# Three PSUM banks for the unit sums of a graph layer, and twelve selection matrices

## The reference

```python
xn = layernorm(x)
gathered = edge_weight[:, None] * xn[dst]                  # graph branch
support = segment_sum(gathered, src, 3125)
graph = relu(concat([xn, support], 1) @ W + b)
mix = mixing(xn)          # logmap, 256 -> 768 projection, batch norm, relu, 32-channel groups,
                          # a linear attention in each node, 512 -> 256 projection, expmap
x = x + graph + mix
x = x + experts(layernorm(x))      # 8 experts, the best two of each node, 256 -> 1024 -> 256
```

## Time and profile before

| | |
|---|---|
| median of 3 runs | 1258.03 us (1256.99 to 1260.42) |
| the profiled execution | 1260.42 us, of which 1260.4 us lie between its first and its last instruction |
| busy | PE 1002.4 us (80%), PEld 810.6, DVE 680.7, POOL 630.3, ACT 598.6 |
| POOL, the 397 gathers (L560) | 394.4 us busy, 994 ns each; idle before them 221.9 us, of it 113.3 for SP's line 455 |
| PE, the unit sums (L705) | 282.1 us busy, 453 ns per instruction; idle before them 164.5 us |

### The profile page before, as it was taken

One profiled execution on the slowest core, in us unless ns is written; L12 is line 12 of the kernel. 1 busy time (PEld: TensorE's weight loads), 2 busy tenths in 40 slices (PEclk: granted clock), 3 DMA queues, 4 the chain that ended last, 5 costly groups with the idle time before them and its releaser, 6 DMA issues.

```text
span 1260.4 us, 21882 instructions
## 1 busy us (share of the span) xinstructions
PE 1002.4 (80%) x5493; PEld 810.6 (64%) x5494; DVE 680.7 (54%) x1493; ACT 598.6 (47%) x1559; POOL 630.3 (50%) x601
## 2 busy tenths in 40 slices
PE   3889579975676777776767557469999999999995
PEld 1456345554555566565655435368999999999995
DVE  8999834432555555555555357943444444444441
ACT  0535234459656676676666445323333343333331
POOL 2473376665666666566666662213433433433431
PEclk8889789996787888789788867778999999999998
DMA  7112222322222222223222343972222222222221
GB/s 157 36 30 84 59 88 88 91 90 80 88 80 87 85 85 88 80 89 90 83 87 85 92 155 122 368 228 48 35 41 35 34 42 34 34 42 34 36 41 18
DMA packets 53869, 103.07 MB, mean 82 GB/s; under 512 B 14923, under 2 KB 36240, under 8 KB 51612
## 3 DMA queue, kind: packets, MB, share of 16 engines
q0 software_dynamic: 30448, 67.69, 21.4%
q1 hardware_dynamic: 22408, 30.48, 7.8%
q10 hardware_dynamic: 932, 3.95, 0.9%
HBM read 83.96 MB, written 18.13 MB: 81 GB/s over the span
## 4 chain that ended last, share of the span: by engine, by line
PE 50%; DVE 14%; another core or an unknown queue 11%; issue 9%; ACT 7%; SPq 3%; DMA 2%; POOL 2%; DVEq 1%; ACTq 0%; POOLq 0%
PE ps L848 15%; PE ps L838 15%; PE ps L705 10%; ACT arena_e L939 3%; PE ps L753 3%; PE ps L716 2%; DVE arena_a L1262 2%; DVE arena_a L1256 2%; DVE arena_c L1343 1%; SPq L454 1%; PE ps L828 1%; POOL arena_c L560 1%; PE ps L648 1%; PE ps L625 1%
## 5 line engine op out<-in xcount | busy, mean ns | idle before, releaser
L560 POOL DMA_INDIRECT arena_c<-y_d,arena_e x397 | 394.4, 994 | 221.9 <-SPq L455 113.3
L705 PE MATMUL ps<-arena_c,arena_e 128*125 x892 | 282.1, 453 | 164.5 <-SPq L458 56.4
L705 PEld LDWEIGHTS ps<-arena_c,arena_e 128*125 128x125 f32 x892 | 184.4, 222 | 243.6 <-issue 218.9
L939 ACT ACTIVATE arena_e<-arena_e 128x125 f32<-128x125 bf16 x446 | 202.3, 509 | 119.2 <-remote 64.6
L1343 DVE TENSOR_TENSOR arena_c<-arena_c,ps 125x256 f32 x223 | 92.6, 415 | 269.2 <-remote 150.3
L592 POOL DMA_INDIRECT out<-node,bn x56 | 100.9, 1802 | 250.8 <-DVE node L1626 225.5
L1065 ACT ACTIVATE arena_d<-ps,small 128x128 f32<-128x128 f32 x448 | 121.5, 382 | 181.8 <-PE ps L838 140.6
L848 PE MATMUL ps<-arena_c,arena_d 128*128 x896 | 205.5, 383 | 0.2 <-issue 0.2
L848 PEld LDWEIGHTS ps<-arena_c,arena_d 128*128 128x128 f32 x896 | 167.9, 192 | 21.7 <-issue 0.6
L838 PEld LDWEIGHTS ps<-node,arena_d 128*128 128x128 f32 x896 | 105.8, 194 | 2.6 <-DVE node L1618 1.2
L838 PE MATMUL ps<-node,arena_d 128*128 128x128 f32 x896 | 106.1, 277 | 0.8 <-DVE node L1618 0.8
(11 more groups left out here) (344 smaller groups left out, 1319.8 us busy)
## 6 DMA issues: line engine op xcount, KB each, us to landing
arena_a<-in_W SPq DMA_DIRECT2D x8, 1024.0 KB, 12.2
arena_c<-y_d,arena_e POOLq DMA_INDIRECT x397
arena_c<-in_W SPq DMA_DIRECT2D x5, 1024.0 KB
arena_c<-in_W ACTq DMA_DIRECT2D x3, 1024.0 KB
x<-in_x SPq DMA_DIRECT2D x5, 560.0 KB
z_d<-x SPq DMA_DIRECT2D x5, 560.0 KB
out<-x SPq DMA_DIRECT2D x5, 560.0 KB
y_d<-arena_c SPq DMA_DIRECT2D x15, 125.0 KB
```

What stands on the lines that cost most here:

```text
L560: pool.indirect_dma_start(ring[:, b % GR, :], None, io["y_d"], bass.IndirectOffsetOnAxis(gix[:, at:at + 1], 0)).then_inc(gth[b % GR], 16)
L705: mm = nc.tensor.matmul(unit_sums(u), sel[(2 * u + j) % SR], ring[:, ds(at + j, 1), :].rearrange("p a c -> p (a c)"), start=(j == 0), stop ...
L939: nc.scalar.activation(sel[b % SR], hot[b // 8 % 2][:, :, b % 8], ACT.Copy, scale=wcols[:, b:b + 1]).then_inc(selm, 1)
```

## The change

From unit 42 on, when the projection no longer needs bank 5, the unit sums rotate through banks 5, 6 and 7, and a unit waits for the add of the unit three before it. `mix_out` gives up bank 5 and writes the columns 256 to 511 of bank 3, whose other half `channel_sums` writes. Two waits go with that: `channel_sums(t)` waits for the store of `mix_out(t-4)`, and `mix_out(t)` waits for the squares of `channel_sums(t+3)`, the one issued last. There are twelve selection matrices in place of eight, and `select` runs eight matrices ahead in place of six. Before unit 42, PE waits until ACT has read the last projection out.

```diff
-SR = 8
+SR = 12
...
-        sel = [cut(T) for _ in range(SR)]
+        sel = [cut(T) for _ in range(8)]
+        cut = cutter(ED[:, 2108:2656])
+        sel += [cut(T) for _ in range(4)]
+        assert len(sel) == SR
...
+        mix_sum = ps[0:T, 3, C:2 * C]
+
         def unit_sums(u):
-            return ps[0:T, 6 + u % 2, 0:C]
+            return ps[0:T, 6 + u % 2 if u < G0 else 5 + (u - G0) % 3, 0:C]
...
-                need(pe, g_acc, u - 1)
+                need(pe, g_acc, u - 1 if u < G0 else u - 2)
...
+            pe.wait_ge(qk_act, OC * 7)
             for u in range(G0, G1):
                 sum_edges(u)
...
             def channel_sums(t):
                 pe.wait_ge(bd_ready, 1)
                 need(pe, a_s, t)
+                need(pe, a_out, t - 3)
...
             def mix_out(t):
                 pe.wait_ge(a_oT, t + 1)
+                need(pe, a_s, min(t + 4, NT))
                 need(pe, a_out, t)
                 for k in range(4):
-                    mm = nc.tensor.matmul(ps[0:T, 5, 0:C], oT[t % 2][:, k, :], wres[:, k, :],
+                    mm = nc.tensor.matmul(mix_sum, oT[t % 2][:, k, :], wres[:, k, :],
...
-            AH = 6
+            AH = 8
...
-                                     ps[0:T, 5, 0:C].rearrange("p (q c) -> p q c", q=4), ACT.Copy).then_inc(a_out, 1)
+                                     mix_sum.rearrange("p (q c) -> p q c", q=4), ACT.Copy).then_inc(a_out, 1)
```

## The result

The changed kernel takes 1267.8 us (median of 4 runs, 1265.68 to 1270.5) against 1257.76 us of the kernel before beside it (1256.99 to 1260.42): ratio 1.0083, 95% interval [1.0058, 1.0108]; a ratio is estimated from the runs and need not be the quotient of the medians. It is 10 us slower, where I forecast 11 us faster. The profiled executions span 1267.5 and 1260.4 us.

What follows compares the result with a forecast made beforehand. The mixing stretch was taken as bound by a circle of waits: POOL, PE, SP and POOL again. 24 - 6 (capped) - 7 = 11 us gained, from 1258.03 to 1247 us; range of 8 in 10: 1224 to 1268.

Steps and rivals of the forecast that it cites:

- The step that failed first: After the last unit: nothing is touched, so gain or loss in the mixing stretch only shifts the experts as a whole.
- rival C: Slower: completions held before both `mix_out` and `channel_sums`, two POOL waits a segment, 50 in all; 1277 us, chance 0.22.
- dry spells: Mixing stretch: POOL's waits for freed slots, 57 of 1.54 us each, 87.9 us, one for 2.7 units.
- The first term, 24 us: Third bank in the mixing stretch: 3.7 units per POOL wait instead of 2.7, 42 waits instead of 57, 24 us less.
- The cap: At `mix_out`: savings between `channel_sums` and `mix_out` can't pass the squares; half of that half kept, so 24 becomes 18 us.
- the wait: `mix_out` waiting for the squares: five tiles lose 2.8 us each, 14 us on PE; bounds 0 and 14, taken as 7.
- rival B: No change: in the mixing segments waiting moves from adds to squares, POOL runs dry 57 times as before; 1258 us, chance 0.16.
- twelve matrices: ACT's selects: more matrices made ahead may let ACT reach its copies sooner; gain taken as 0.
- `channel_sums` waits 1.4 us for the store: `channel_sums` waiting for the store: covered by 0.9 us, taken as 0; at most 39 us if the cover is gone.
- the signs that I named for "right": Mixing stretch: POOL's waits some 45, unit-sum idling well below 117.7 us, `mix_out` idling 1 to 3 us a tile, three units held.
- held completion: Mixing stretch: PE's completions reach nobody for about five microseconds while gathers follow each other, arriving after POOL runs dry.

Runs made afterwards that it cites:

- e8: Changed kernel plus three throwaway matmuls behind each of its last six units and one in each of the first eight logits tiles: 1249.41 us, 0.9977 of the kernel before.
- e5: Changed kernel as it is, run again beside a fresh set of the kernel before: 1259.94 us, ratio 1.0061.
- e14: Changed kernel with mixing sums in bank 4, `mix_out` moved behind the row transposes, and two banks throughout: 1253.72 us, 0.9942 of the kernel before.
- e13: Changed kernel with mixing sums in bank 4, `mix_out` moved, three banks in the mixing segments, two in the tail: 1249.63 us, 0.9900 of the kernel before.
- e7: Kernel before, two banks and eight matrices, with the mixing sums in bank 3 and all the new waits: 1258.76 us, ratio 1.0047.
- e1: Changed kernel plus three throwaway matmuls behind each of its last five units: 1249.42 us, 0.9949 of the kernel before.
- e4: Changed kernel with eight matrices, six ahead, so the third bank and its waits alone: 1261.97 us, 1.0056 of the kernel before.
- e9: Changed kernel with its last 16 units back on two banks, three banks and all waits kept in the mixing segments: 1251.2 us, 0.9977 of the kernel before.
- e11: Kernel before, two banks and eight matrices, with mixing sums in bank 4 and `mix_out` moved behind the row transposes: 1243.63 us, ratio 0.9907.
- e2: Kernel before plus three throwaway matmuls behind each of its last five units: 1251.64 us, ratio 0.9974.
- e3: Kernel before with twelve selection matrices, eight made ahead, and its two banks: 1253.67 us, ratio 1.0003.
- e12: Changed kernel, mixing sums in bank 4, `mix_out` moved, throwaway matmuls behind the last units, in the logits loop and before the experts: 1238.48 us, 0.9869 of the kernel before.

## Why the prediction was wrong

**The step that failed first** is the sentence "The change touches nothing after the last unit; what it gains or loses here shifts the experts as a whole." No instruction after the last unit is changed, but the clock at which they run is: the way from the last add to the first expert takes 10.1 us more, of which the experts give 2.1 back, and the two profiled spans are 7.1 us apart. e8 against e5 shows it by holding the clock (10.5 us). My rival C ended on the right side, 1277, by a mechanism that did not happen: idle time before `channel_sums` is 1.4 us, and POOL has fewer dry spells, not as many.

**The first term, 24 us, was mis-sized.** I took POOL's dry spells as proportional to the units that PE finishes in one, 2.7 with two banks and 3.7 with three. e14 has 48 with two banks and e13 47 with three, at 4.1 us less; the rule held only from one bank to two. In the place that the change gives `mix_out`, the third bank is worth 3 to 4 us of the stage (e7 against e1, e4, e5, e8 and e9). (My product was off by one as well: 15 x 1.54 is 23, not 24.) Two banks with `mix_out` moved had 41 or 48 in this stretch (e11, e14), so the 57 of the earlier trace rows were not the banks' number.

**The cap and the wait.** I kept 18 of the 24 us and took 7 off for `mix_out`. The price of the waits alone came out near that, 6.1 us (e7), by luck: not five tiles that lose 2.8 us, but 17 waits of 1.6 us. The cap was the mistake of kind: I let half of the units keep their gain, and what happened in the segments is rival B, "The waiting moves from the adds to the squares: PE stands at `mix_out` till the same release". 117.7 us became 44.9 + 72.3. POOL's 57 dry spells did not stay, as B had it, but the eight fewer brought the stage 0.2 us. So 18 - 7 = 11 us was, in the stage, some 3 to 4 less 5: about nothing, and e8 beside e2 finds no gain in the total with the clock held either.

**What held:** twelve matrices are worth 0 (e3), though ACT's idle time before the selects fell from 98.4 us to 16.0 there; `channel_sums` waits 1.4 us for the store. Of the signs that I named for "right", PE's idle time before the unit sums fell, POOL's waits came to 49, near my 45, and `mix_out` got idle time of its own, though 3.3 us a tile in place of my 1 to 3. Three finished units waited for a held completion, too: of the 99 adds from 309 to 738 us that began more than 1 us after their unit was done, 25 found three units done; before there were never more than two. The signs were there and the kernel was slower, because all of them are signs of one stage.

**Open:** what makes the clock fall at the border in one execution and not in another. That PE stands before the loop is not enough to explain e1 and e13. The kernel before may lose the clock there, too. Beside e5 to e8 its 28 runs lie in two groups, 17 at 1248.0 to 1253.6 us with a mean granted clock of 0.878 to 0.890, and 11 at 1256.2 to 1263.2 us with 0.872 to 0.877; the first two profiles, one with the fall and one without, have 0.872 and 0.882. If so, the change makes the fall more frequent and is not its only cause; that is not shown, since only profiled executions show the loop. Beside e9 to e12 nine of the 17 runs have 0.882 to 0.889, as the runs of e11 do (0.886 to 0.893), and a median of 1250.96 us: against these e11 gains 7.3 us, and not 11.8. Also open is why moving `mix_out` helps the kernel with two banks. Whether the half bank is to be had without its waits was not tried.

## What to carry to other kernels

When a buffer is bought with a wait, add up the idle time of the waiting engine before and after, over all its lines: if the sum stays, the wait has only moved. Check the granted clock on both sides of each border between phases, since a change that ends one phase differently can set the clock, and the time, of the next one that nobody touched. And where a phase of small matmuls follows, filler that reaches into it can hold the clock: 26 short matmuls were worth 10.5 us here. One profile shows one execution: where a level can fall in some and not in others, look at the spread of the runs before you call a fall the change's.

## What the runs showed of the hardware

A busy PE did not bring the clock back within the loop: in the changed kernel the loop ran at 0.50 with PE busy 18.00 of 18 us, while the same loop, entered at 1.00, kept 1.00 with PE busy 16.48 us in the kernel before (in e3, e8 and e12 it fell about 1 us before the loop ended). The Trainium skill ("TensorE: Matmul & The Clock Gate", section "Part 4: PE-mode transpose") says that transposes don't count as a busy TensorE in the way that matmuls do, and that full clock doesn't engage for them. The loop at 0.50 fits that but does not test it, since each tile has as many matmuls as transposes; the loop at 1.00 shows that transposes need not end it at once.

The same kernel spread over up to 21 us on one chip (e1, 1241.5 to 1262.9 us), and with `mix_out` in its old place the stage was 3 to 9 us shorter in the experiments (462.6 to 467.8 us) than in the first pair of profiles (471.3 and 471.1).
